# Matmuls on zeros in front of two groups of transposes, in the last layer norm and second feed-forward of a two-layer metaformer

## What is computed

```python
def _ln_t(v, eps=1e-05):
    m = jnp.mean(v, axis=-1, keepdims=True)
    s = jnp.var(v, axis=-1, keepdims=True)
    return (v - m) / jnp.sqrt(s + eps)

def _L1_ffn_ref(h, gate_w, gate_b, w1, b1, w2, b2):       # 8 experts, 64 -> 256 -> 64
    C = max(1, math.ceil(CAPACITY_FACTOR * T / E))         # 160 slots for each expert
    logits = x @ gate_w + gate_b
    probs = jax.nn.softmax(logits, axis=-1)
    idx = jnp.argmax(probs, axis=-1)
    ...
    pos = (jnp.cumsum(one_hot, axis=0) * one_hot).sum(-1).astype(jnp.int32) - 1
    kept = pos < C
    buf = jnp.zeros((E, C, D), dtype=h.dtype).at[idx, pos_safe].set(x, mode='drop')
    hmid = jax.nn.relu(jnp.einsum('ecd,edf->ecf', buf, w1) + b1[:, None, :])
    ybuf = jnp.einsum('ecf,efd->ecd', hmid, w2) + b2[:, None, :]
    y_tok = ybuf[idx, pos_g] * (prb * kept)[:, None]
...
t = t + _L1_ffn_ref(_ln_t(t), ...)
```

## Time and profile before

| | |
|---|---|
| median of 3 runs | 347.27 us (346.35, 347.27, 351.0) |
| the profiled execution, its own time | 348.37 us |
| its span, first to last instruction | 346.6 us |
| mean granted TensorE clock over the span | 0.842 |
| PE, PEld, DVE, ACT, POOL busy | 245.3, 135.8, 224.6, 54.9, 170.4 us |

### The profile page before, as it was taken

How to read it: one execution, slowest core, us unless ns; L and a number is a source line. 1 busy time by engine, 2 the same in 40 slices (tenths; PEclk the granted TensorE clock), 3 DMA queues, 4 the chain that set the end, 5 groups by cost and what they waited for, 6 DMA issues and landing times.

```text
span 346.6 us, 2786 instructions
## 1 busy us (share of the span) xinstructions
PE 245.3 (71%) x832; PEld 135.8 (39%) x834; DVE 224.6 (65%) x480; ACT 54.9 (16%) x91; POOL 170.4 (49%) x198
## 2 busy tenths in 40 slices
PE   1976869868496899999988385668696876028600
PEld 1642636423142653222353142346374745016600
DVE  7758999799989447336430859999988044601307
ACT  1309700000000117221311100001010203002200
POOL 5801773299769143911100599799993010440062
PEclk9989698998879569999999679699989696557955
DMA  4477910000000000000018200000000000010011
GB/s 156 118 146 152 204 32 0 0 1 0 0 1 0 3 0 0 0 2 2 0 30 179 48 1 2 1 0 1 0 2 0 0 0 3 11 55 2 19 37 42
DMA packets 7882, 10.82 MB, mean 31 GB/s; under 512 B 4280, under 2 KB 4792, under 8 KB 7801
## 3 DMA queue, kind: packets, MB, share of 16 engines
q1 hardware_dynamic: 7354, 10.12, 12.7%
q0 software_dynamic: 512, 0.53, 0.6%
HBM read 8.03 MB, written 2.61 MB: 31 GB/s over the span
## 4 chain that ended last, share of the span: by engine, by line
DVE 32%; PE 29%; issue 17%; POOL 8%; ACT 1%; DMA 1%; DVEq 1%; POOLq 0%; ACTq 0%
DVE ps L1464 8%; PE ps L827 5%; DVE ring L295 4%; PE ps L752 4%; DVE ring L1194 4%; PE ps L787 4%; POOL ring L266 3%; PE ps L861 3%; PE ps L715 3%; POOL slots_in L562 2%; DVE ps L274 2%; DVE big L1468 1%; DVE ring L288 1%; PE ps L696 1%; PE ps L794 1%
## 5 line engine op out<-in xcount | busy, mean ns | idle before, releaser
L266 POOL TENSOR_TENSOR ring<-big 128x384 f32<-128x384 f32 x72 | 58.6, 845 | 4.8 <-DVE ps L1464 3.7
L886 PE MATMUL ps<-ring,ident 128*128 128x384 f32 x78 | 32.1, 545 | 14.8 <-POOL ring L266 10.5
L295 POOL TENSOR_TENSOR ring<-big 128x512 f32<-128x512 f32 x25 | 35.2, 1438 | 12.5 <-issue 6.5
L696 PE MATMUL ps<-zero,ident 128*128 128x512 f32 x38 | 27.5, 884 | 16.8 <-DMA slots_in<-xn,idx_in 15.2
L765 PE MATMUL ps<-ring,ident 128*128 128x512 f32 x62 | 33.3, 687 | 7.2 <-DVE ring L295 5.8
L1464 DVE TENSOR_TENSOR ps<-ps,ring 128x384 f32<-128x384 f32 x57 | 32.0, 562 | 6.4 <-PE ps L886 2.7
L433 POOL TENSOR_TENSOR rstd<-veps,mhalf 128x4 f32<-128x4 f32 x8 | 8.3, 1041 | 52.0 <-DVE veps L1021 52.0
L752 PE MATMUL ps<-ring,ident 128*128 128x192 f32 x78 | 27.7, 527 | 7.9 <-DVE ring L288 4.4
L288 POOL TENSOR_TENSOR ring<-big 128x576 f32<-128x576 f32 x10 | 17.2, 1727 | 27.5 <-DVE big L1098 16.9
L886 PEld LDWEIGHTS ps<-ring,ident 128*128 128x128 f32 x78 | 14.5, 205 | 28.6 <-DVE ring L266 8.5
L752 PEld LDWEIGHTS ps<-ring,ident 128*128 128x128 f32 x78 | 18.5, 241 | 17.1 <-DVE ring L288 5.6
(11 more groups left out here) (265 smaller groups left out, 407.3 us busy)
## 6 DMA issues: line engine op xcount, KB each, us to landing
big<-pad SPq DMA_DIRECT2D x8, 392.0 KB, 9.1
big<-pad SPq DMA_DIRECT2D x8, 240.0 KB, 5.8
w<-in_w_dram SPq DMA_DIRECT2D x1, 520.0 KB
w<-in_w_dram SPq DMA_DIRECT2D x1, 512.0 KB
pad<-img SPq DMA_DIRECT2D x8, 64.0 KB, 2.1
pad<-zero SPq DMA_DIRECT2D x1, 484.0 KB, 3.9
pad<-zero SPq DMA_DIRECT2D x1, 400.0 KB, 4.5
slots_in<-zero SPq DMA_DIRECT2D x1, 320.0 KB, 4.8
```

The source lines that it names most:

```text
L266: return eng.tensor_tensor(V(ring, 0, slot * SP, [[1, P], [NJ * C, 3], [C1, NJ * G1], [1, C1]]), bigv((py + dy) * SLAB1 + (dx + j0) * C, [ ...
L295: return eng.tensor_tensor(V(ring, 0, slot, [[1, P], [C0, J * G0], [1, C0]]), bigv(wy * SLAB0 + wx * C, [C0, J * G0], [1, C0]), bigv(AW + ...
L696: mm(bank(free_bank, 0, P, [1, 512]), ident[:, :], zero[:, 0:512], start=True, stop=True)
L886: mm(bank(1 + i % 2, 0, P, [1, SP]), ident[:, :], ring[:, slot * SP:slot * SP + SP], start=(n == 0), stop=(n == len(srcs) - 1)).then_inc(s ...
```

## The change

Two calls are left out, 5 matmuls, 10 records. Nothing is put in their place.

```diff
             last.then_inc(sem("x3_ps"), 1)
 
 
-            keep_clock(3, 4)
             transposes(5, normalised, "xn", 3)
             pe.wait_ge(sem("w_ffn1"), 64)
             project(w_g1[:, :], 4, E, "gate_ps", 5, slot=E)
...
             pe.wait_ge(sem("scattered"), 16 * J)
-            keep_clock(2, 6)
             pe.wait_ge(sem("slots_loaded"), 16)
             for i in range(ST_N):
                 last = tr(bank(i // 4, 0, C, [1, P], off=(i % 4) * P), bigv(XS + i * C, [1, C]), ident[:, :])
```

## The result

The changed kernel took 354.15 us (median of 4 runs: 352.48, 354.06, 354.24, 354.27). In this comparison the kernel before took 348.72 us (346.35, 347.27, 350.16, 351.0). The ratio is 1.0149 with a 95% interval of 1.0076 to 1.0223: slower, by an amount that the interval places on either side of 2%. In a later comparison with more runs, 12 of the changed kernel against 35 of the one before, the medians were 353.41 and 351.26, 2.2 us apart (1.006), and the ratio was 1.0111, from 1.0046 to 1.0176. The ratios leave out runs that are over 1.5% above the fastest of their kernel, which in the later comparisons is about half of the runs of before, while the medians are of all runs. The forecast was 349.4 us, with a range from 346.8 to 351.1.

What follows compares the result with a forecast made beforehand. The last 65 us were taken as one chain with hardly any overlap, PE bounding the expert layers. Terms +0.3 - 0.5 + 2.3 = +2.1 us on the median 347.27 gave 349.4 us, range 346.8 to 351.1.

Steps and rivals of the forecast that it cites:

- What bounds the kernel: Last 65 us: one chain through the engines with hardly any overlap; PE bounds the expert layers, 316.73 to 325.83.
- First edit, its matmuls: Zeros beside the layer norm: covered, with 1.70 us of PE idle behind them, so leaving them out saves 0.
- First edit, the clock: Transposes of xn and gate: clock falls earlier, second four transposes slower, gate unchanged; +0.3 us, from 0 to +1.1.
- Second edit, the start: Transposes of the slots: the first starts at 312.87 in place of 313.35, saving 0.5 us, bounds 0 and 0.6.
- Second edit, the clock of the experts: Hidden layer starts at the lower clock, which returns 3.7 to 6.2 us later; +2.3 us, from 1.7 to 2.9.
- What would show it: Profile signs: clock 0.50 at the hidden layer's start, that layer 6 to 7.5 us, slots' transposes within 0.2 us of landing.
- The sum: Whole kernel: +0.3 - 0.5 + 2.3 = +2.1 us, at least -0.4 and at most +4.0.
- How the numbers follow: Whole kernel: chances given to forecast and rivals; median of few runs of before off by about half a us.
- the clock comes back without help: Rival at the hidden layer: full clock there after the ten transposes and short wait; 346.8 to 347.5 us, chance 0.15.
- the clock stays low to the end of the experts: Rival at both expert layers: lower clock throughout, +8.2 us in all, 355.5 us, chance 0.05.
- the matmuls on zeros don't do what their name says: Rival at both edits: some executions of before already lose clock, so removal changes less; 347.3 to 348.5 us, chance 0.13.

Runs made afterwards that it cites:

- the ordered kernels: Kernel before and changed kernel, each with POOL's memset of w_ob made to wait for VectorE's first tap: 347.67 us with both calls, 351.01 us with neither.
- the forced ones: Kernel before and changed kernel, VectorE's first tap made to wait until POOL's long memset is about to begin: 350.68 us with both calls, 353.48 us with neither.
- Zeros behind the transposes: One matmul on zeros of 288 columns added after the ten transposes, to the changed kernel with POOL's w_ob memset waiting for the first tap: 347.50 us.
- early variant: Kernel before with POOL's w_ob memset waiting for the first tap; second call enlarged to five matmuls, started when half the scatters have landed: 347.53 us.

## Why the prediction was wrong, point by point

**What bounds the kernel.** Right for the part that it speaks of. Wrong in what it left out: it read the time before from one profile and three runs as if a run of this kernel were that profile with small noise. The kernel has two usual times, by the meeting at 12.4 us: the 17 runs under 349 have a median of 346.5, the 80 others one of 351.3; the profile and two of the three runs were of the rarer one. The three runs spread over 4.6 us, and the text put this down to half a us of doubt about a median.

**First edit, its matmuls: 0.** Right; the profile after shows PE idle 4.33 us in their place.

**First edit, the clock: +0.3 (0 to 1.1).** 0.25 in the profile after; with this call alone left out 0.1 from L947 on, +0.3 between medians. The first four transposes cost nothing and the gate nothing, as worked out. The second four took 1.06 us where 1.12 had been put. The gate's 16 weight loads took 3.54 us at the lower clock again. The one time that the Trainium skill, page "TensorE: Matmul & The Clock Gate", section "LDWEIGHTS (loading the stationary operand)", gives for a weight load does not fit that and the 1.86 us of the earlier trace rows both, as the prediction said.

**Second edit, the start: -0.5.** 0.7 in the profile after, 0.6 of it the transposes' place and 0.1 the load's landing (first weight load 2.86 us after its issue against 2.99).

**Second edit, the clock of the experts: +2.3 (1.7 to 2.9).** 2.9 in the profile after (7.50 against 4.61); the layer took 7.40 to 7.50 us in the four other profiles that had neither the second call nor zeros behind the transposes. The price of the lower clock was sized well, the time at it was at the upper end of the 3.7 to 6.2: the clock came back 5.7 to 5.9 us after the layer's start in all five. The signs named under "What would show it" came as they were told, the 7.50 us at the edge.

**The sum: +2.1.** The edits cost 3.3 us between the medians of the ordered kernels, 2.8 between the forced ones, 2.2 between those of the later comparison, and 2.2 to 2.6 between profiles from L947 on. So the sum was right in its mechanism and 0.1 to 0.5 us short by the profiles. From a before with the meeting, 351.3 us, it would have given 353.4, and twelve more runs of the changed kernel gave 353.41.

**The step that failed** is therefore the one under "How the numbers follow": the runs of before taken as a centre with half a us of doubt, and with it the carrying of 347.27 into the sum. The text gave the meeting no term at all. By their times the changed kernel's four runs had the meeting, and two of the three of before had not. The size of the meeting is shown by forcing it (350.68) and by taking it away (347.67): 3.0 us. With 2.2 to 3.3 for the edits, 347.3 becomes 352.5 to 353.6; the four runs, at 354.15, lay another 0.5 us or more above that, which no trace explains. The upper end of the range, 351.1, missed them by 3 us. That the kernel before has the meeting in most of its runs could not be seen in one profile, but two kinds of run could be seen in 346.35, 347.27 and 351.0.

**The rivals.** That the clock comes back without help happened in none of the profiles; whether the transposes did anything towards it stays open, as said under "Zeros behind the transposes". What is shown is that transposes run at the full clock where it is granted: the early variant's ten took 1.25 against 2.31 us. There the traces disagree with the Trainium skill, page "TensorE: Matmul & The Clock Gate", "Part 4: PE-mode transpose", which says that the full clock doesn't engage for them. That the clock stays low to the end of the experts happened nowhere. That the matmuls on zeros don't do what their name says is out for the second call; the first keeps the clock up for the first transposes only (0.60 against 1.04 us), and that is worth next to nothing here.

## What to carry to other kernels

Look at the spread of the few runs before trusting their median: 4.6 us over three runs was two kinds of run, and the profile showed only one. When two executions are compared, measure the stretch of the edit by itself, from a fixed instruction ahead of it. A matmul on zeros is best placed in a wait that PE has anyway between two pieces of work; there one of 288 columns did nearly what two of 512 in front did (0.4 to 0.8 us short in its profile, level by medians). It is not enough that the clock is up when work begins: count what PE does in the us before and behind it too.

## What the runs showed of the hardware

A tensor_scalar of VectorE on float32 in SBUF and POOL's memsets stopped each other here. The first tap ended about 0.3 us behind a memset each time (13.01 - 12.69, the end of POOL's cw_parts before; 0.30 and 0.32 us behind the last memset in two other profiles), and lasted 2.85 to 3.64 us when it had to wait for the memset of big. Not every VectorE instruction does so: seven scalar_tensor_tensor of the same size took 5.92 us where the memset of big stood beside the first few and 5.91 where it didn't, and the memset took 2.71 us in both. The Trainium skill, page "SBUF — State Buffer", "Who interferes with whom", says that VectorE and GpSimd share a port pair under an exclusive lock, that a tensor_scalar can run in a mode that takes the pair, and that then the one that issues later waits for the other's whole instruction. The traces agree for one memset; no row names the mode. They add that the wait need not end with that memset: in the profile after, the tap waited through seven more that began after it. Who gets the port when it is freed differed between executions with the same order of instructions; what decides it was not found.
